# The last bias of a two-layer network: laid into the result's PSUM bank by ScalarE instead of added to the rows by GpSimd

## What is computed

```
x = x + L0_xattn(layernorm(x), ctx)          # 16 heads
x = x + L0_ffn(layernorm(x))                 # mixture of 8 experts, top 2, layernorm of its result
x = x + L1_xattn(layernorm(x), ctx, mask)    # one head, masked
x = x + L1_ffn(layernorm(x))

def L1_ffn(x, weight, bias):
    xq, xs = mx_quantize(x)        # blocks of 32, scale = max|x| / 7.5, nearest value of an fp6 grid
    wq, ws = mx_quantize(weight)
    return (xq * xs) @ (wq * ws).T + bias
```

## Time and profile before

| | us |
|---|---|
| median of three runs | 1045.76 |
| lowest and highest of the three | 1042.63, 1046.62 |
| the profiled execution's own time | 1037.06 |
| its span, first to last instruction | 1035.3 |
| busy in the span: PE, weight loads, DVE, ACT, POOL | 946.8, 808.0, 529.4, 509.2, 515.6 |
| mean granted TensorE clock, as a share of full speed | 0.971 |

### The profile page before, as it was taken

The page is one execution under the profiler, slowest core; times in us unless marked ns, Lnnn a source line. Parts: engine busy times, 40 slices in busy tenths (PEclk is TensorE's granted clock), DMA queues, the critical chain, the costliest instruction groups (busy, mean ns, idle before and its releaser), DMA issues.

```text
span 1035.3 us, 22010 instructions
## 1 busy us (share of the span) xinstructions
PE 946.8 (91%) x7131; PEld 808.0 (78%) x7131; DVE 529.4 (51%) x1276; ACT 509.2 (49%) x1292; POOL 515.6 (50%) x675
## 2 busy tenths in 40 slices
PE   6999999989876887999999999999999999798776
PEld 4767777666646777899999999999999998676654
DVE  4677898877762332443323232232323223899871
ACT  4776777766643442334333333333333333577663
POOL 2524343655643075656444443434444442688873
PEclk9999999999998998999999999999999999999897
DMA  4264454655643455434322212222121227333210
GB/s 142 81 167 158 133 167 125 154 123 138 158 113 92 151 113 107 36 55 59 51 38 41 37 31 37 34 39 39 34 42 31 42 40 192 111 92 98 86 42 31
DMA packets 90734, 89.58 MB, mean 87 GB/s; under 512 B 19808, under 2 KB 85792, under 8 KB 90496
## 3 DMA queue, kind: packets, MB, share of 16 engines
q1 hardware_dynamic: 74944, 69.48, 23.6%
q0 software_dynamic: 15680, 18.69, 12.3%
HBM read 56.74 MB, written 31.39 MB: 85 GB/s over the span
## 4 chain that ended last, share of the span: by engine, by line
PE 44%; DVE 7%; issue 5%; DMA 3%; POOL 3%; ACT 2%; POOLq 0%; SPq 0%; DVEq 0%; ACTq 0%
PE b_H L1515 20%; PE b_Y L1527 20%; DMA ffn_rows<-b_y,b_slots 2%; POOL buckets L405 2%; DVE c_x_bn L1975 2%; PE c_f_ps L2227 1%; PE b_xT L1504 1%; ACT c_probs L2142 1%; DVE c_centred L1988 1%; ACT c_xn L2097 1%; DVE c_x L2065 1%; DVE c_amax L2045 1%; POOL b_rows L1449 1%; DVE c_nmax L2036 1%; DMA c_ctx<-in_ctx 0%
## 5 line engine op out<-in xcount | busy, mean ns | idle before, releaser
L1684 ACT ACTIVATE b_hiddenT<-b_H,b_b 128x128 f32<-128x128 f32 x568 | 162.5, 369 | 325.5 <-PE b_H L1515 325.5
L1515 PEld LDWEIGHTS b_H<-b_rowsT,b_w 128*128 128x128 f32 x2272 | 266.6, 193 | 4.8 <-ACT b_rowsT L1691 1.1
L1515 PE MATMUL b_H<-b_rowsT,b_w 128*128 128x128 f32 x2272 | 267.4, 276 | 0.5 <-ACT b_rowsT L1691 0.4
L1527 PE MATMUL b_Y<-w_sb,b_hiddenT 128*128 x1136 | 263.0, 386 | 0.0
L1460 POOL DMA_INDIRECT ffn_rows<-b_y,b_slots x71 | 141.8, 1998 | 216.0 <-DVE b_y L1620 141.9
L1527 PEld LDWEIGHTS b_Y<-w_sb,b_hiddenT 128*128 128x128 f32 x1136 | 214.9, 194 | 27.5
L1616 DVE TENSOR_TENSOR b_y<-b_Y,b_b 128x256 f32<-128x256 f32 x71 | 30.1, 425 | 329.9 <-PE b_Y L1527 320.6
L1605 DVE COPY b_w<-w_sb 128x2048 f32 x71 | 87.6, 1234 | 32.2 <-issue 26.0
L1206 ACT COPY a_probsT<-a_T 120x512 f32<-120x512 f32 x128 | 74.9, 585 | 46.6 <-PE a_T L911 40.7
L1449 POOL DMA_INDIRECT b_rows<-xn_rows,b_slots x71 | 75.7, 1066 | 43.2 <-issue 20.8
L405 POOL DMA_INDIRECT buckets<-r_pay,r_place x64 | 68.1, 1064 | 53.9 <-DVE r_place L398 28.6
(11 more groups left out here) (222 smaller groups left out, 1315.8 us busy)
## 6 DMA issues: line engine op xcount, KB each, us to landing
w_sb<-in_L_ffn_W SPq DMA_DIRECT2D x32, 512.0 KB, 4.1
a_xin<-in_x SPq DMA_DIRECT2D x16, 256.0 KB, 3.1
a_xres<-in_x SPq DMA_DIRECT2D x32, 128.0 KB, 4.7
x_rows<-a_x SPq DMA_DIRECT2D x32, 128.0 KB, 1.7
xn_rows<-a_xn SPq DMA_DIRECT2D x32, 128.0 KB, 2.7
shared_rows<-a_shared SPq DMA_DIRECT2D x32, 128.0 KB, 2.8
b_spare<-shared_rows SPq DMA_DIRECT2D x16, 256.0 KB, 4.7
ffn_rows<-b_spare SPq DMA_DIRECT2D x16, 256.0 KB, 3.7
```

The source lines that it names most:

```text
L1515: j = pe.matmul(H_ps[i][:, c * P:(c + 1) * P], w1c[i][:, k * HID + c * P:k * HID + (c + 1) * P], xT[:, k * P:(k + 1) * P], start=(k == 0), ...
L1527: j = pe.matmul(y_ps[i][:, 0:D], hT[i][:, c * P:(c + 1) * P], w2_sb[:, bass.ds(e * (HB * D) + c * D, D)], start=(c == 0), stop=(c == HB - 1))
L1684: j = act.activation(hT[i][:, c * P:(c + 1) * P], H_ps[i][:, c * P:(c + 1) * P], ACT.Gelu, bias=b1c[i][:, c:c + 1])
```

## The change

ScalarE copies the bias, spread over the tile, straight from SBUF into `c_f_ps` (`lay_bias(c - 1)`, placed after `keep_result(c - 2)` and ahead of `keep_context` and `round_blocks`). `start_result` then reads x4 itself and adds onto the bank (`start=False`). GpSimd's `add_bias` and the two `x4b` tiles go. DVE's wait for `x4b` becomes a wait for `linear(n - 2)`. So that the products add onto the bank and don't overwrite it, one product with `start=True` is put ahead of PE's loop, whose values the first `lay_bias` overwrites.

```diff
@@ POOL
-            def add_bias(n):
-                pool.wait_ge(s_x4, n + 1)
-                ge(pool, s_f_p, n - 1)
-                pool.tensor_tensor(x4b[n % 2][:], x4[n % 2][:],
-                                   fb[:].unsqueeze(1).broadcast_to(T2), ALU.add
-                                   ).then_inc(s_x4b, 1)
...
-                add_bias(c - 1)
@@ DVE, attended
-                ge(dve, s_x4b, n - 1)
+                ge(dve, s_f_p, n - 1)
@@ ACT
+            def lay_bias(n):
+                if not exists(n):
+                    return
+                if n == 0:
+                    act.wait_ge(second["s_vec"], 32)
+                    act.wait_ge(s_fb, 1)
+                ge(act, s_o, n)
+                act.copy(f_ps[:], fb[:].unsqueeze(1).broadcast_to(T2)).then_inc(s_fb, 1)
...
                 keep_result(c - 2)
+                lay_bias(c - 1)
@@ PE, start_result
-                pe.wait_ge(s_x4b, n + 1)
-                ge(pe, s_o, n)
+                pe.wait_ge(s_x4, n + 1)
+                pe.wait_ge(s_fb, n + 2)
                 pe.matmul(f_ps[:].rearrange("p u d -> p (u d)"), ident[:],
-                          x4b[n % 2][:].rearrange("p u d -> p (u d)"),
-                          start=True, stop=False, skip_group_check=True)
+                          x4[n % 2][:].rearrange("p u d -> p (u d)"),
+                          start=False, stop=False, skip_group_check=True)
@@ PE, ahead of the loop
+            pe.matmul(f_ps[:].rearrange("p u d -> p (u d)"), ident[:],
+                      wdT[:].rearrange("p k d -> p (k d)"), start=True, stop=True,
+                      skip_group_check=True).then_inc(s_fb, 1)
```

More of the change, by code:

```diff
@@ L1760, in second_phase @@
         pT = ring("c_probsT", [P, 2, P], n=2)
-        x4, xn4, x4b = ring("c_x4_", T2, n=2), ring("c_xn4_", T2, n=2), ring("c_x4b", T2, n=2)
+        x4, xn4 = ring("c_x4_", T2, n=2), ring("c_xn4_", T2, n=2)
         am, sc, rsc = (ring("c_amax", [P, 2 * NB], n=2), ring("c_scale", [P, 2 * NB], n=2),
@@ L1833, in second_phase @@
         s_xn4 = sem("c_xn4_ready")
-        s_x4b = sem("c_x4_bias")
+        s_fb = sem("c_result_bias_set")
         s_am = sem("c_amax_ready")
@@ L1929, in inverse_std @@
                                        ).then_inc(g.s_r, 1)
-            def add_bias(n):
-                if not exists(n):
-                    return
-                pool.wait_ge(s_x4, n + 1)
-                ge(pool, s_f_p, n - 1)
-                pool.tensor_tensor(x4b[n % 2][:], x4[n % 2][:],
-                                   fb[:].unsqueeze(1).broadcast_to(T2), ALU.add
-                                   ).then_inc(s_x4b, 1)
             def to_blocks(n):
```

## The result

Over 20 runs each the changed kernel took 1037.84 us (median, 1033.51 to 1044.65) and the kernel before 1042.74 (1036.36 to 1046.62). The ratio is 0.9955, 95% interval 0.9938 to 0.9972: 4.7 us less (2.9 to 6.5), where 1.4 less was forecast. The three runs known when the prediction was made, 1045.76, lay 3 us above the later median. The time was outside the range given, 1040 to 1048.

The account below looks back on a forecast made before the run. VectorE was taken to set the pace mid-phase. Rounds gaining 1.75 us less 0.35 for the product ahead of the loop gave 1.40 less: 1044.4 us from a median of 1045.76, range 1040 to 1048.

Parts of the forecast that it names:

- `c_scale` waits for GpSimd's addition: On VectorE in a round like the seventh, removing GpSimd's addition cuts c_scale from 0.42 to 0.17 us.
- The length of the rounds: VectorE's rounds: 7.7 to 7.75 us in rounds 6 to 8, about 7.95 in rounds 2, 3 and 5.
- The product ahead of the loop: On TensorE before the loop, the added product starts the loop 0.35 us later, bounds 0 and 1.02.
- The step that failed: Slow products in rounds 9, 11 and 13 stay; these rounds lose 0.08 (9 and 11 together) and 0.45 us (13).
- Its 0.25 vanishes in that wait: In rounds 9 and 11 VectorE waits 1.27 us after a slow product, which swallows the 0.25 us saved.
- losses of 0.08 and 0.45 from the copy: ScalarE's copy delays c_q and the next c_z: 0.04 us each in rounds 9 and 11, 0.45 in round 13.
- round 14: On VectorE in round 14, c_scale falls from 0.62 to 0.17 us, a gain of 0.45.
- the clock falls less often: Rival: two fewer slow TensorE products, or full clock in the last ones; 1039 to 1042 us, chance 0.15.
- The sum: Over the whole kernel: 1.75 us gained in the rounds less 0.35 for the added product, 1.40 us less.
- The range: Measured time of the whole kernel between 1040 and 1048 us, with 2 in 10 left outside.
- The signs: Expected in the trace: about 1.7 us of GpSimd idle time before c_vq, and four products above 3 us.

Follow-up runs that it names:

- before_third: The kernel before, unchanged, traced a third time; one trace only, with a span of 1035.3 us in the first trace and 1026.0 us here.
- after_third: The changed kernel, unchanged, traced a third time and timed against the kernel before: ratio 0.9947.
- copy_only_second: Second run of the kernel before with GpSimd's addition kept and ScalarE's copy added, which start_result then overwrites: ratio 0.9998 to the kernel before.
- after_no_start: The changed kernel without start_result's product, its waits kept and the residual left out of the result: ratio 1.0058 to the kernel before.

## Why the prediction was wrong

- **`c_scale` waits for GpSimd's addition**: right. It takes 0.17 or 0.18 in all 16 rounds of each trace of the changed kernel, and in `no_add`, where the addition is gone and no copy takes its place (what else changes there are two waits and the tile that TensorE reads).
- **The length of the rounds**: right, but for rounds 9, 11, 13 and 14 (below). Undisturbed traces stand against each other in before_third and after_third: 7.98 to 7.73 in round 1, 7.99 to 7.95 and 8.03 in rounds 2 and 3, 8.29 to 8.00 in round 4, 7.98 to 7.99 in round 5, 7.98 to 7.78 in round 6, 7.97 to 7.99 against 7.73 or 7.74 in rounds 7 to 12. ScalarE does hold the early rounds, by a copy of 0.59 (0.62 assumed) behind which the next instruction does not start 0.09 before its end in round 7, as I had it, but 0.03 after it. The later `c_q` costs VectorE time on a second path that the prediction doesn't have. GpSimd's `c_xd` waits for `c_q` and then runs into VectorE's `centre`, which takes 1.14 to 1.15 us in rounds 2 to 5 where it takes 0.93 to 0.96 in the other rounds that have it. Round 2 of the changed kernel, then round 7, VectorE and GpSimd from their own timelines:

```profile
920.21 1.14 DVE L1978 SCALAR_TENSOR_TENSOR c_centred<-c_acc,c_acc_mv,c_gamma 128x256 f32<-128x256 f32 x2
919.63 1.05 POOL L1946 TENSOR_TENSOR c_xd<-c_q,c_amax 128x512 f32<-128x512 fp8e4 x1 [0.17 <-ACT c_q L2150]
...
959.94 0.96 DVE L1978 SCALAR_TENSOR_TENSOR c_centred<-c_acc,c_acc_mv,c_gamma 128x256 f32<-128x256 f32 x2
959.18 1.04 POOL L1946 TENSOR_TENSOR c_xd<-c_q,c_amax 128x512 f32<-128x512 fp8e4 x1
```

In both rounds `centre` ends 0.67 to 0.68 us after `c_xd`. In the early rounds the scores end only 0.04 us ahead of `c_z` as well, so both paths end there together, and by these rows freeing one alone would gain under 0.1.

- **The product ahead of the loop**: about 0.5 on average (0.24 against the first trace of before), forecast 0.35; within its bounds of 0 and 1.02, and it depends on how long TensorE would have waited there without it.
- **The step that failed is that of rounds 9, 11 and 13**: "Its 0.25 vanishes in that wait", and losses of 0.08 and 0.45 from the copy. It carried the four slow products of one trace over as if they were part of the program. They are in two traces of three of the kernel before and in none of the seven traces of the changed kernel and of its versions that keep all its products. Where they are absent on both sides, rounds 9 and 11 gain 0.25 each, round 13 gains 0.55 (8.22 to 7.67; its `c_scale` falls from 0.73), round 14 gains 0.05 and not 0.45, and nothing is lost. These four rounds give 1.10 where the prediction's terms add up to -0.08. In all it is 118.65 us from the first `c_z` to the last in before_third, 115.83 in after_third: 2.8 less, not 1.75. The rival "the clock falls less often", held at 0.15, was the nearer case.
- **The sum**: the four ratios, weighted by their intervals, give 0.9957, within about 0.0011: 4.5 us, within 1.2. The rounds explain 2.8, and the product takes back 0.5, so 2.3 is accounted for. The other 2 or so would be one or two slow products (1.27 us of waiting each) per execution on average, and the higher mean clock of the changed kernel (by 0.0017, 0.0053 and 0.0045 where both are known) points the same way. But a clock raised by 0.0038 in copy_only_second brought no time, so that share is inferred, not shown.
- **The range** was also set 3 us too high, by hanging it on a median of three runs: hung on the later 1042.74 it would have been 1037 to 1045 and held the 1037.84, with the failed step all the same.
- **The signs**: for the idle time ahead of `c_vq` the text says about 1.7, but its own terms (0.47 + 1.27 - 0.25) give 1.49, and 1.46 was measured. Four products above 3 us were expected; the traces of the changed kernel have one or none, the last, and the trace of before had five with its last.

What stays open: why one trace of the kernel before has four slow products and another none, with equal gaps; and why a mean clock raised by 0.0038 in copy_only_second brought no time.

## What to carry to other kernels

When an engine's work is taken away and it wasn't the bound, look for a short instruction on the bounding engine that ends just as that work ends: here 20 us of GpSimd's busy time counted for nothing by themselves, and 0.25 us per round of a 128x16 VectorE instruction made the part of the gain that is shown. Before a clock drop in one trace is put into a sum as a fixed cost, take a second and a third trace of the same kernel. And before an instruction is moved, list who waits for it, not only who waits behind it.

## What the runs showed of the hardware

- A VectorE instruction on a 128x16 tile that takes 0.17 us by itself took 0.22 to 0.73 where it began while GpSimd's 1.27 us addition was running. It ended 0.02 to 0.04 us after it in each of rounds 1 to 14 of before and before_third.
- VectorE's `centre`, which reads two tiles in SBUF, took 0.84 to 0.88 us where no `c_xd` of GpSimd was running at its start. It took 0.93 to 0.97 where `c_xd` ran on for 0.25 to 0.30 us, and 1.14 to 1.16 where it ran on for 0.45 to 0.49. The changed kernel still has this wait in nearly all rounds.
- Less work for TensorE made the kernel slower: without `start_result`'s product the ratio to the kernel before was 1.0058 (1.0029 to 1.0087), with five slow products ahead of the last. The Trainium skill (TensorE: Matmul & The Clock Gate, "HAM oscillation — how this bites in real kernels") tells of the clock falling where a wait for a DMA takes up much of each tile. Here it fell in rounds of 8 us with two waits of 1.4 to 1.5 us each for ScalarE; how much of it those waits bring is not shown, since gaps of 0.65 and 1.44 us stood in a trace with slow products and in one without.
- In after_no_start the scores began 0.35 to 0.37 us after the copy that they waited for, in the rounds from the second on; in the kernel before and in the changed one it was 0.09 to 0.15. TensorE's idle time ahead of them doesn't explain it by itself: it was 0.91 us or more in after_no_start, but 0.85 in one round of the kernel before, which had 0.10. The cause is open.
